# Linear attention written with transposed outputs in column tiles, and its gate projection as one FP32r pass

## What is computed

```
def step(S, inp):
    qt, kt, vt, gt = inp
    S = S * jnp.exp(gt)[..., None] + kt[..., :, None] * vt[..., None, :]
    ot = jnp.einsum('bhk,bhkv->bhv', qt, S)
...
q = (hidden_states @ Wq).reshape(B, T, H, DK) * scale
k = (hidden_states @ Wk).reshape(B, T, H, DK)
v = (hidden_states @ Wv).reshape(B, T, H, DV)
gk = jax.nn.log_sigmoid(hidden_states @ Wgk0 @ Wgk1 + bgk1) / GATE_NORM
o = _gla_core(q, k, v, gk)
g = (hidden_states @ Wg).reshape(B, T, H, DV)
o = o * jax.lax.rsqrt(jnp.mean(o * o, axis=-1, keepdims=True) + EPS)
o = o * g_norm_w * (g * jax.nn.sigmoid(g))
return o.reshape(B, T, H * DV) @ Wo
```

## Time and profile before

| | us |
|---|---|
| median of 3 runs | 1974.85 |
| these runs | 1974.85, 2499.33, 1969.23 |
| the profiled execution | 1982.53 |
| its span in the trace | 1980.8 |
| linear attention in it, from its first load to its last matmul | 309 to 816.4 |

### The profile page before, as it was taken

The page is one execution under the profiler, slowest core; times in us unless marked ns, Lnnn a source line. Parts: engine busy times, 40 slices in busy tenths (PEclk is TensorE's granted clock), DMA queues, the critical chain, the costliest instruction groups (busy, mean ns, idle before and its releaser), DMA issues. The chain is left out here.

```text
span 1980.8 us, 27666 instructions
## 1 busy us (share of the span) xinstructions
PE 1691.0 (85%) x7766; PEld 1143.3 (58%) x7766; DVE 1127.5 (57%) x2746; ACT 752.5 (38%) x1820; POOL 747.2 (38%) x850
## 2 busy tenths in 40 slices
PE   6869995599899889787899477879999999998798
PEld 4545564257565667554566356645566666664677
DVE  6832222656646463486222288947776666755588
ACT  5523331515142331353333311116665655644221
POOL 3534435332333010153444366405554555544000
PEclk9979996878978778688999778879999999999899
DMA  6119995110111000230799322200000000000000
GB/s 201 62 46 274 284 270 174 29 40 25 32 32 32 1 0 1 80 96 1 223 297 286 116 78 78 62 0 1 1 1 1 1 1 1 1 1 1 6 19 19
DMA packets 82776, 142.27 MB, mean 72 GB/s; under 512 B 15240, under 2 KB 42736, under 8 KB 82688
## 3 DMA queue, kind: packets, MB, share of 16 engines
q1 hardware_dynamic: 52992, 90.81, 15.4%
q0 software_dynamic: 15360, 37.77, 6.8%
q10 hardware_dynamic: 14336, 12.59, 2.2%
HBM read 122.25 MB, written 18.87 MB: 71 GB/s over the span
## 5 line engine op out<-in xcount | busy, mean ns | idle before, releaser
L2210 POOL TENSOR_TENSOR sb_m_prob<-sb_m_prob,sb_m_rinv 128x512 f32<-128x512 f32 x256 | 258.7, 1042 | 289.0 <-DVE sb_m_rinv L2259 289.0
L2166 ACT ACTIVATE sb_m_prob<-m_ps_s,sb_m_nmax 128x512 f32<-128x512 f32 x256 | 173.8, 684 | 204.0 <-DVE sb_m_nmax L2263 204.0
L2263 DVE TENSOR_REDUCE sb_m_nmax<-m_ps_s 128x2 f32<-128x1024 f32 x128 | 156.4, 1222 | 127.9 <-PE m_ps_s L2061 127.8
L1237 POOL DMA_INDIRECT sb_c_rows<-slot_rows,sb_c_at x192 | 197.6, 1029 | 74.8 <-issue 48.8
L1216 DVE TENSOR_TENSOR sb_e_h<-sb_e_sg,e_ps_gu 96x176 f32<-96x176 f32 x128 | 42.7, 333 | 269.0 <-ACT sb_e_sg L1192 269.0
L1154 PE MATMUL e_ps_gu<-e_wgu,sb_e_xT 128*96 128x352 f32 x512 | 178.4, 471 | 19.7 <-ACT sb_e_xT L1186 19.5
L1129 POOL DMA_INDIRECT sb_e_x<-xn_rows,sb_e_index x128 | 121.4, 949 | 102.9 <-POOL sb_e_index L103 96.5
L2069 PE MATMUL m_ps_p<-sb_ident,sb_m_prob 128*128 128x128 f32 x1024 | 136.3, 273 | 15.8 <-ACT sb_m_pT L2174 11.3
L2069 PEld LDWEIGHTS m_ps_p<-sb_ident,sb_m_prob 128*128 128x128 f32 x1024 | 117.8, 141 | 41.2 <-POOL sb_m_prob L2210 13.8
L1171 PE MATMUL e_ps_y<-e_wdn,sb_e_hT 96*96 96x256 f32 x512 | 132.2, 381 | 0.0
L1251 DVE SCALAR_TENSOR_TENSOR sb_x<-sb_c_rows,sb_weight,sb_x 128x256 f32 (+1 forms) x192 | 95.4, 497 | 61.2 <-DMA sb_c_rows<-slot_rows,sb_c_at 56.2
(11 more groups left out here) (268 smaller groups left out, 3642.2 us busy)
## 6 DMA issues: line engine op xcount, KB each, us to landing
e_wgu<-wgu SPq DMA_DIRECT2D x128, 352.0 KB, 4.7
e_wdn<-wdn SPq DMA_DIRECT2D x128, 192.0 KB, 4.5
slot_rows<-sb_e_y ACTq DMA_DIRECT2D x128, 96.0 KB
xn_rows<-sb_r_xn SPq DMA_DIRECT2D x16, 256.0 KB, 2.2
sb_c_rows<-slot_rows,sb_c_at POOLq DMA_INDIRECT x192, 2.8
sb_x<-x SPq DMA_DIRECT2D x4, 512.0 KB, 5.5
sb_e_x<-xn_rows,sb_e_index POOLq DMA_INDIRECT x128, 4.8
sb_g_zm<-wqT SPq DMA_DIRECT2D x1, 2048.0 KB, 9.4
```

The source lines that it names most:

```text
L1237: pool.indirect_dma_start(rows[u][j][:, :], None, k.slot_rows[:, :], bass.IndirectOffsetOnAxis(ap=at[u][:, j:j + 1], axis=0))\
L2166: act.activation(prob[s % 4][:, hh, :], ps_s[s % 2][:, hh, :], ACT.Exp, bias=nmax[s % 2][:, hh:hh + 1], accum_out=rsum[s % 2][:, hh:hh + 1 ...
L2210: pool.tensor_tensor(part, part, rinv[s % 2][:, hh:hh + 1].to_broadcast([P, T]), ALU.mult)\
L2263: dve.tensor_reduce(nmax[s % 2][:, :], ps_s[s % 2][:, :, :], AX, ALU.max, negate=True).then_inc(nmax_ready, 1)
```

## The change

- **Outputs.** `state_mid` and `v` become the stationary operands, with 32 columns, and the tokens are the 128 moving ones. The four heads of a group write to partitions 0, 32, 64 and 96 of `ps_o`, so each is a 128x32 column tile. The result has values on the partitions. At j=0 the state is zero, so its matmuls are gone; at j=3 `ps_kv` and the state's update are gone.
- **Norm.** ACT copies `o` and writes its square; PE multiplies the square by a matrix `same_head` of ones per head (`mean_squares`, a new unit in the three banks); ACT takes Ln and Exp of all 128x256 sums. POOL's squares and DVE's reduction go. `normed(j)` runs on DVE one iteration later. The transposes of `output` and ACT's copy behind them go. `g_norm_w` is multiplied into `wo0` once. POOL makes `gw` with one operation in place of three.
- **Gates.** `Wgk0` and `Wgk1` lie three times on partitions 0, 32 and 64, as high part, low part of the weights, and low part of the input: z is one FP32r matmul for each head in place of an FP32 one. DVE makes the low part (`low_parts`), and PE waits for it. ACT writes |z| beside z (two activations for each head), and DVE's `absolute` goes.
- **Rest.** v and the output gates are separate units. The `e_` factors have two buffers, and DVE's copies of them go. The hardware loop is written out.

```diff
@@ load_attention_weights
-    sp.dma_start(k.wgk0[:, :, 0:LR], w["wgk0"].rearrange("(c p) n -> p c n", p=P)).then_inc(loaded_w0, 16)
-    sp.dma_start(k.wgk1[0:LR, :], w["wgk1"]).then_inc(loaded_w0, 16)
+    for at in range(0, 3 * LRS, LRS):
+        sp.dma_start(k.wgk0[:, :, at:at + LR], w["wgk0"].rearrange("(c p) n -> p c n", p=P)).then_inc(loaded_w0, 16)
+        sp.dma_start(k.wgk1[at:at + LR, :], w["wgk1"]).then_inc(loaded_w0, 16)
...
@@ PE
             def output(b, j):
...
-                for c in range(2):
-                    ins = pe.transpose(to[:, c * P:(c + 1) * P], flat[:, c * P:(c + 1) * P], k.ident[:, :])
-                given(ins, stage, ("o", j))
-                emptied(pe, stage, ("o", j))
-                pe.wait_ge(out_used, b * TB + (j + 1))
+                if n:
+                    pe.wait_ge(out_used, n)
                 for c in range(2):
-                    ins = pe.matmul(ps_out[:, :], oT[:, c, :], k.wo0[:, c, :], start=(c == 0), stop=(c == 1))
+                    ins = pe.matmul(ps_out[:, :], on[:, c, :], k.wo0[:, c, :], start=(c == 0), stop=(c == 1))
                 ins.then_inc(out_ready, 1)
...
+            def mean_squares(b, j):
+                pe.wait_ge(sq_ready, b * TB + j + 1)
+                to = take("ms", b, j)
+                given(pe.matmul(to[:, 0:2 * SUB], same_head[:, :], sq[:, :, :].rearrange("p i t -> p (i t)"),
+                                start=True, stop=True), "ms", b, j)
...
-                    for h in range(H0):
-                        pe.matmul(ps_o[:, h, :], qp[:, h, tokens], state_mid[j % 2][:, h, :], start=True, stop=False)
-                        ins = pe.matmul(ps_o[:, h, :], atm[:, h, :], v[:, j, h * DV:(h + 1) * DV],
-                                        start=False, stop=True)
+                    for i in range(2):
+                        if j:
+                            for h in range(i * HG, (i + 1) * HG):
+                                at = h % HG * DV
+                                pe.matmul(ps_o[at:at + DV, i, :], state_mid[j % 2][:, h, :], qp[:, h, tokens],
+                                          start=True, stop=False)
+                        for h in range(i * HG, (i + 1) * HG):
+                            at = h % HG * DV
+                            ins = pe.matmul(ps_o[at:at + DV, i, :], vb[:, j, h * DV:(h + 1) * DV], atm[:, h, :],
+                                            start=(j == 0), stop=True)
                     ins.then_inc(o_ready, 1)
                     if j:
-                        output(b, stage, j - 1)
+                        output(b, j - 1)
+                    mean_squares(b, j)
                     after[j]()
...
@@ ACT
+                    act.activation(za[:, h, :], src[:, :], ACT.Abs, bias=k.bgk1[:, h:h + 1]).then_inc(abs_ready, 1)
                     act.activation(zm[:, h, :], src[:, :], ACT.Identity, bias=k.bgk1[:, h:h + 1])\
...
-                act.activation(o[j % 2][:, :, :], ps_o[:, :, :], ACT.Copy).then_inc(o_copied, 1)
+                act.activation(o[j % 2][:, :, :], ps_o[:, :, :], ACT.Copy)
+                act.activation(sq[:, :, :], ps_o[:, :, :], ACT.Square).then_inc(sq_ready, 1)
...
@@ DVE
+            def low_parts(b):
+
+                rest = slice(2 * LRS, 3 * LRS)
+                dve.wait_ge(low_ready, b + 1)
+                src = use(dve, "low", b, 0)
+                dve.tensor_tensor(low[rest, :], src[rest, :], low[rest, :].bitcast(F32), ALU.subtract)\
+                   .then_inc(low_split, 1)
...
+                        normed(b, j - 1)
                     begin[j]()
                     if j >= 2:
                         add_out(b, j - 2)
```

More of the change, by code:

```diff
@@ L1422, in low_rank @@
                 for c in range(DC):
                     ins = pe.matmul(to[:, :], k.wgk0[:, c, :], xT[:, c, :], start=(c == 0), stop=(c == DC - 1))
-                given(ins, stage, ("low", 0))
-            def gates(stage, heads):
-                emptied(pe, stage, ("low", 0))
-                for h in heads:
-                    to = take(stage, ("z", h))
-                    given(pe.matmul(to[:, :], k.wgk1[:, h * DK:(h + 1) * DK], low[:, :], start=True, stop=True),
-                          stage, ("z", h))
@@ L1433, in first_gates, with gates @@
-            def first_gates(stage):
-                low_rank(stage)
-                gates(stage, range(HG))
-            def values_gates(stage, tiles):
-                for j in tiles:
-                    to = take(stage, ("vg", j))
+                given(ins, "low", b, 0)
+            def gates(b, heads):
+                pe.wait_ge(low_split, b + 1)
+                if b == 0:
+                    pe.wait_ge(w_low, 1)
+                for h in heads:
+                    to = take("z", b, h)
+                    given(pe.matmul(to[:, :], wgk1[:, h * DK:(h + 1) * DK], low[:, :], start=True, stop=True), "z", b, h)
@@ new lines, in values, with output_gates @@
+            def values(b):
+                for half in range(2):
+                    to = take("v", b, half)
+                    for i in range(2):
+                        j = 2 * half + i
+                        for c in range(DC):
+                            ins = pe.matmul(to[:, i * VW:(i + 1) * VW], xT[:, c, j * P:(j + 1) * P], k.wvg[:, c, 0:VW],
+                                            start=(c == 0), stop=(c == DC - 1))
+                    given(ins, "v", b, half)
+            def output_gates(b):
+                for i in range(2):
+                    to = take("g", b, i)
@@ L1593, in lns @@
+                act.activation(part, part, ACT.Exp, scale=-1.0).then_inc(exp_steps, 1)
             def lns(b, half):
                 part = za[:, half * HG:(half + 1) * HG, :]
-                act.wait_ge(act_steps, b * 2 + (half + 1))
+                act.wait_ge(exp_steps, b * 2 + half + 1)
                 act.activation(part, part, ACT.Ln, bias=1.0).then_inc(soft_ready, 1)
-            def vg_copies(stage, tiles):
-                for j in tiles:
-                    src = use(act, stage, ("vg", j))
-                    act.activation(sig[:, j, :], src[:, VW:2 * VW], ACT.Exp, scale=-1.0)
-                    act.activation(vg[:, j, :], src[:, :], ACT.Copy).then_inc(freed(stage, ("vg", j)), 1)
@@ L1605, in sigmoids, with value_copies @@
-            def sigmoids(b, stage):
-                for j in range(TB):
-                    emptied(act, stage, ("vg", j))
+            def value_copies(b):
+                for half in range(2):
+                    src = use(act, "v", b, half)
+                    act.activation(v[b % 2][:, 2 * half:2 * half + 2, :].rearrange("p j n -> p (j n)"), src[:, :], ACT.Copy)\
+                       .then_inc(freed("v", b, half), 1)
+                emptied(act, "v", b, 0)
+                emptied(act, "v", b, 1)
+                act.sem_inc(v_ready, 2)
```

596 lines of the change are left out of this document (293 added, 303 removed).

## The result

| | before | after |
|---|---|---|
| median of four runs, us | 1976.0 | 1916.4 |
| ratio, 95% interval | | 0.968 (0.960 to 0.977) |
| the profiled execution, us | 1982.5 | 1916.0 |
| first scores to last output of linear attention | 393.3 | 330.9 |

Each side had one execution far longer than its others (2499.3 and 3193.6 us), which is in the median and not in the ratio.

The account below looks back on a forecast made before the run. PE was taken to bound the recurrences, partly at 1.2 GHz. Savings of 39 us (three recurrences), 17.4 (the last) and 1 (projections) sum to 57.4: 1917.5 us against the median 1974.85, range 1897 to 1943.

Parts of the forecast that it names:

- Outputs at 1.0 us: A chunk's outputs on PE: four tiles side by side plus 0.14 us, 1.0 us in all, 0.6 at j=0.
- Rival 4: Outputs slower: each tile's record waits for the whole flow through the array; 65 us lost, 1982 us; chance 0.03.
- z waits for ACT: Chunks 0 and 1: ACT's two activations a head set the pace, so PE's saved 5.0 us are spent waiting.
- PE waits 5 and 9 us: Chunks 2 and 3: PE idles 5 and 9 us at two output products, as DVE's `log_gates` precedes `add_out`.
- The walk: A recurrence timed from its first scores: scores of chunk 2 at 31.6 us, q at 65.
- What bounded behind the faster outputs: Skill's PSUM rule weighed: evacuation may bound, limiting gain to what ACT and DVE leave; already counted through `log_gates`.
- Projections of batch 0: The stage's first stretch, 114.1 us: 1 us less, between 3 less and 3 more.
- Last recurrence 40.5: The bare last recurrence, four chunks and a tail: 40.5 us in place of 57.9, 17.4 less.
- q and k phases unchanged: Three q and k phases: no gain; POOL's gathers set 34.3 and 35.0 us, FP32 matmuls take 27.5 of 32.0.
- Rival 1: Output tiles run one after another: outputs cost 2.4 us more, 23 us given back, 1941 us; chance 0.12.
- Rival 2: ACT bounds more: 3 us more ahead of DVE in chunks 1 and 2, 18 in all, 1936 us; chance 0.17.
- Rival 3: The clock holds in the recurrences: 4 us a round and 5 at the end gained, 1900 us; chance 0.12.

Follow-up runs that it names:

- z_fp32: The changed kernel with z made by one FP32 matmul for each head again, without the split weights: 1920.6 us, ratio 0.968 to the kernel before.
- abs_dve: The changed kernel with the absolute value of z moved from ACT back to DVE: 1905.0 us, ratio 0.961 to the kernel before.
- unrolled: The kernel before with only its hardware loop over rounds 0 and 1 written out: ratio 0.999 to the kernel before.
- quad: The changed kernel with the outputs computed four times over in each chunk: 1933.9 us, ratio 0.975 to the kernel before.
- tiles: The changed kernel with the same 16 output matmuls ordered column tile by column tile: 1907.5 us, ratio 0.970 to the kernel before.

## Why the prediction was right, point by point

The measured median lies 1.1 us from the forecast. That closeness is luck: single executions of the changed kernel spread by 17 us, and terms that were off by 2 to 4 us cancelled. The mechanism is what was right.

- **Outputs at 1.0 us.** Right: 1.0 (0.65 at j=0) against 1.0 and 0.6, from the pair of the earlier trace rows. Four tiles side by side cost 0.15 us beyond their share of 0.86, the pair 0.14. On the change of tiling mode: the product behind the outputs starts 0.33 us after their last group, and a group takes 0.22, so leaving the mode costs at most 0.11 here. The Trainium skill, "TensorEngine Tiling (Array Packing)", Key Properties, names a drain and no price; the row gives it one. Rival 4, in which the tiles' records wait for each other, is out.
- **z waits for ACT.** Right, and stronger than put: `z_fp32` shows that the pass earned nothing, `abs_dve` that the second activation is what costs.
- **PE waits 5 and 9 us.** Right: 4.65 and 9.89. The walk was 0.5 to 2.3 us too long up to the scores of chunk 2 (31.6 against 29.3, 31.1, 30.5) and 1.5 too short from there to q (33.4 against 35.0, 34.7, 34.9). The two nearly cancelled in 65, which was luck. The second has a place: in chunk 2 DVE reached `log_gates` 4.2 us after the scores began (451.59 to 455.77), where the walk had 2.6 (1.8 and two operations of 0.41).
- **What bounded behind the faster outputs.** DVE and ACT did, though not by taking the tiled product out of PSUM (two activations of 0.38 us): by gate work queued ahead of a short `add_out`. The Trainium skill, "TensorEngine Tiling (Array Packing)", PSUM Bottleneck, says that tiling speeds up TensorE and not the evacuation of PSUM. The trace bears out that the next bound lies on the engines behind PE, and not that it is the evacuation.
- **Projections of batch 0.** Wrong in sign, inside the stated 3: 0.9 more in place of 1 less. DVE's two `log_gates` did get 3.0 shorter (21.35 in place of 24.33), but they begin 64.6 us after the stage's first load in place of 60.7, 3.9 later, where I had put 2 for ACT's activations. Counted from 309 in both traces the stretch looks 0.8 shorter, because the stage ahead ended 1.7 sooner in this execution; between the profiles of this study that end varies by 9 us.
- **Last recurrence 40.5.** It was 38.4; a chunk took 8.6 to 11.4 in place of 8.2 to 11.7. The same instructions took from 32.3 to 38.4 in the profiles of this study, so the term had a spread of 6 us of its own (granted clocks 1.00 to 0.82), which the sum did not carry.
- **q and k phases unchanged.** The step that was wrong: a term put at nothing. They lost 1.2, 1.7 and 1.4. In round 2 I had priced the missing transposes and ACT's copy at 0.9 for each `output`, and then gave the phase nothing, though `output(3)` stands in it: from the end of the twelve q records ahead of it to the next q matmul it took 1.8 (733.22 to 735.04) and takes 0.9 (690.46 to 691.32). Another 0.5 is clock, in the first twelve q records (6.9 against 6.4). In rounds 0 and 1, 0.8 and 0.5 come from the loop written out (`unrolled`); the rest of their 1.2 and 1.7 was not taken apart.
- **The way into the next stage** lost 2.1 us, which no step had. The profiled executions differ by 66.5, 9.1 beyond the forecast's 57.4: 4.3 by the phases, 2.1 by the last recurrence, 2.1 here, 2.9 outside the stage (1.7 ahead of it, 1.2 behind), less 1.9 by the projections and 0.4 by the recurrences. The medians differ by 59.6, and single executions of the changed kernel by up to 17.
- **Rival 1** was not what happened, and its price was wrong: `quad` puts all of the 2.6 us back and costs 9 us of the stage, not 23, and `tiles`, with half of it, nothing that shows. I counted a delay of PE in chunk 1 through to the end. It does reach the scores of chunk 2 (33.5 against 31.0), but PE then idles 2.6 us less ahead of each output product, and the scores that follow ran at the higher clock, which gave it back in round 2.
- **Rival 2** (ACT bounds more) is out. A head's two activations took 1.14 us where the walk had 1.2, the scores of chunk 2 came 0.5 to 2.3 us sooner than in the walk, and the waits for `add_out` were 4.65 and 9.89 us and not 3 longer than forecast.
- **Rival 3** (the clock holds) half came true: granted 0.81 to 0.83 in the recurrences against 0.72 to 0.74. The outputs' runs of 32-column matmuls are gone (the key-value products' remain), but the output products behind the waits of 4.65 and 9.89 us ran at 1.2 GHz.

## What to carry to other kernels

Before you speed up an engine, list what its slow work covers on the others. Then read the queue of the engine that it will wait for: where a short operation that releases it stands behind a long one that nobody needs yet, exchange them in the same change. Here that exchange was worth nothing before the change and 33 us of the stage after it, half of what the change itself brought. And check each part alone: the one-pass projection bought nothing, as its consumer set the pace.

## What the runs showed of the hardware

- Column tiles overlap by their place in PE's queue, and PE starts a matmul on another tile ahead of one that stands before it in the queue (434.67 against 434.89 in `tiles`). Two FP32 matmuls in a row on one tile cost nothing (0.66 us for 16 records); four in a row cut the overlap from four tiles to two (2.4 us for 32 records in place of 1.0). The four hold pairs that add into one place of PSUM, and whether the number or the pairing counts was not run.
- The clock is part of the price of a wait. A wait of 4.66 us was followed by three operations at 1.2 GHz, one of 2.03 us by the same three at 2.4 GHz. And a stretch of unchanged instructions took 32.3 or 38.3 us.
- A burst of POOL's indirect loads can go with a delay of 2 to 4 us on ACT, and in the kernels of one group on DVE too, though both waited for PE alone; in `quad` PE itself paused among matmuls that wait for nothing. It did so in five profiles of eight in which it ran across chunk 0, and in none of three in which it was held back.
